# Value products of a half batch in two long runs instead of four, and one output projection for four batches, in a 16-head cross-attention on Trainium2

## The reference, cut to what matters

```
q = (x @ Wq.T).reshape(b, t, h, s)
k_ = (context @ Wk.T).reshape(b, tc, h, s)
v = (context @ Wv.T).reshape(b, tc, h, s)
dot = einsum('bthd,bchd->bhtc', q * e ** (-0.25), k_ * e ** (-0.25))
attn = softmax(dot, axis=-1)
out = einsum('bhtc,bchd->bthd', attn, v).reshape(b, t, e)
return out @ Wo.T + bo
```

## Time and profile before

| | us |
|---|---|
| median of 3 runs | 2212.78 |
| lowest and highest run | 2210.36 and 2214.60 |
| span of the profiled execution | 2210.2 |
| PE busy in it | 2062.2 (93%) |
| DVE busy in it | 1482.6 (67%) |
| ACT busy in it | 1200.2 (54%) |

### The profile page before, as it was taken

The page is one execution under the profiler, slowest core; times in us unless marked ns, Lnnn a source line. Parts: engine busy times, 40 slices in busy tenths (PEclk is TensorE's granted clock), DMA queues, the critical chain, the costliest instruction groups (busy, mean ns, idle before and its releaser), DMA issues. The chain is left out here.

```text
span 2210.2 us, 47308 instructions
## 1 busy us (share of the span) xinstructions
PE 2062.2 (93%) x18797; PEld 1505.9 (68%) x18797; DVE 1482.6 (67%) x3068; ACT 1200.2 (54%) x2313; POOL 752.7 (34%) x337
## 2 busy tenths in 40 slices
PE   5999999866999899999999999999997799999996
PEld 3677777655887455677777777777764457777774
DVE  5677777688986554566666666666626577777774
ACT  5877887634766222344444444444421467777763
POOL 6565566016875470112111211112000254433410
PEclk8999999967999898999999999999997889999997
DMA  6554544233540311231112211131000354544420
GB/s 161 148 148 132 159 134 132 63 85 97 143 136 20 79 38 39 70 104 66 60 60 82 97 60 60 60 100 62 1 1 25 87 159 126 149 126 139 122 79 9
DMA packets 94541, 199.78 MB, mean 90 GB/s; under 512 B 42113, under 2 KB 50353, under 8 KB 94066
## 3 DMA queue, kind: packets, MB, share of 16 engines
q1 hardware_dynamic: 94322, 196.75, 30.3%
HBM read 116.22 MB, written 0.65 MB: 53 GB/s over the span
## 5 line engine op out<-in xcount | busy, mean ns | idle before, releaser
L1630 PEld LDWEIGHTS L2ps<-L2probsT,L2values 125*128 125x128 f32 (+1 forms) x2688 | 317.4, 192 | 51.3 <-issue 48.9
L1611 PE MATMUL L2ps<-L2keys,L2qz 128*128 128x501 f32 x672 | 340.2, 590 | 0.9 <-DVE L2out_bias L1847 0.9
L1630 PE MATMUL L2ps<-L2probsT,L2values 125*128 125x128 f32 (+1 forms) x2688 | 318.5, 275 | 0.5 <-ACT L2probsT L1740 0.5
L1725 POOL TENSOR_TENSOR L2keys<-L2keys,L2mean_spread 127x1500 f32<-127x1500 f32 x15 | 50.9, 3395 | 583.0 <-DMA L2wqk<-L_moments 583.0
L1823 DVE CUSTOM_DVE_ANT_0 L2work<-L2ps,L2maskadd,L2big 128x1503 f32<-128x1503 f32 x112 | 199.5, 1781 | 72.9 <-PE L2ps L1611 72.7
L1625 PEld LDWEIGHTS L2ps<-const,L2work 128*126 128x126 f32 x1344 | 164.3, 140 | 118.7 <-issue 116.5
L654 ACT ACTIVATE L3probsT<-L3ps 128x448 f32<-128x448 f32 x384 | 196.0, 547 | 71.1 <-PE L3ps L511 66.5
L654 ACT ACTIVATE L0probsT<-L0ps 128x448 f32<-128x448 f32 x384 | 198.1, 551 | 47.7 <-PE L0ps L511 46.6
L1625 PE MATMUL L2ps<-const,L2work 128*126 128x128 f32 x1344 | 202.8, 273 | 3.5 <-DVE L2work L1832 3.1
L1742 ACT COPY L2qz<-L2ps 128x128 f32<-128x128 f32 x112 | 29.7, 265 | 304.7 <-PE L2ps L1630 304.7
L798 DVE TENSOR_REDUCE L0partmax<-L0ps 112x1 f32<-112x1000 f32 x128 | 153.4, 1199 | 58.1 <-PE L0ps L484 56.0
(11 more groups left out here) (479 smaller groups left out, 4164.7 us busy)
## 6 DMA issues: line engine op xcount, KB each, us to landing
L0key_stack<-L0key_parts SPq DMA_DIRECT2D x192, 187.5 KB
L3key_stack<-L3key_parts SPq DMA_DIRECT2D x192, 187.5 KB
L0ctxT<-in_ctxT SPq DMA_DIRECT2D x16, 750.0 KB, 4.4
L1rawT<-in_ctxT SPq DMA_DIRECT2D x16, 750.0 KB, 6.5
L2raw<-in_ctx SPq DMA_DIRECT2D x16, 750.0 KB
L3ctxT<-in_ctxT SPq DMA_DIRECT2D x16, 750.0 KB, 4.4
L2mean_spread<-L_moments SPq DMA_DIRECT2D x15, 750.0 KB, 6.7
L2wqk<-L_moments SPq DMA_DIRECT2D x15, 750.0 KB, 8.4
```

The source lines that it names most:

```text
L1611: last = nc.tensor.matmul(PS[:, 3 * (m % 2) + c, 0:NPR], tile_rows(m), KT[:, m // RT % 2, 500 * c:500 * c + NPR], start=True, stop=True)
L1630: last = nc.tensor.matmul(PS[:, bank, 0:P], V[0:keys_in(c), i // RT % 2, c, :], PT[0:keys_in(c), i % 2, c, :], start=c == 0, stop=c == NCH ...
```

## The change

`values` now does six chunks instead of three, and only in odd steps: half a batch's twelve chunks come in two runs of 24 matmuls each instead of four runs of 12. `pv_done` counts finished half batches instead of quarters. Y takes four batches at once, 224 columns instead of 56, in one step of every fourth batch (t = 0, b = 5, 9, 13 and 17); `Am` has room for four batches and lies in the space of the loaded weights `W`, which aren't needed any more by then. `copy_sums` now stands behind all the exponentials of its step instead of behind the first.

```diff
@@ of_step
-        if t == 0 and 0 <= b - 2 < B:
-            own.append(("Y", b - 2, 0, "D"))
+        if t == 0 and b % 4 == 1 and 0 <= b - 5 < B:
+            own.append(("Y", (b - 5) // 4, 0, "D"))
@@ tiles
-        Am = sb("heads_out", [P, 2, TT])
-        W = sb("w", [P, 6, P])
+        W = sb("w", [P, 7, P])
+        Am = W[:].rearrange("p a n -> p (a n)").rearrange("p (h x b q) -> p h x b q", h=2, x=2, b=4)
@@ values
-                wait_emptied(pe, plan.emptied("S", 4 * h + 3, (3 * part + 2) // 4))
+                wait_emptied(pe, plan.emptied("S", 4 * h + 3, part + 1))
-                for c in range(3 * part, 3 * part + 3):
+                for c in range(6 * part, 6 * part + 6):
-                last.then_inc(s.pv_done, 1)
+                if part == 1:
+                    last.then_inc(s.pv_done, 1)
@@ unit, Y on PE
-                    wait_emptied(pe, plan.emptied("R", 2 * i + 1, 0))
+                    wait_emptied(pe, plan.emptied("R", 8 * i + 7, 0))
-                            last = nc.tensor.matmul(PS[:, bank, 0:Q], WO[:, h, x, :], Am[:, h, x * Q:(x + 1) * Q],
+                            last = nc.tensor.matmul(PS[:, bank, 0:4 * Q], WO[:, h, x, :], Am[:, h, x].rearrange("p b q -> p (b q)"),
@@ PE's steps
-                h, part = n // 4 - 1, n % 4
-                if 0 <= h < HB:
-                    values(h, part)
+                if n % 2 == 1 and 0 <= n // 4 - 1 < HB:
+                    values(n // 4 - 1, n % 4 // 2)
@@ ACT's steps
                 for u in own[:1]:
                     empty(*u)
+                for u in own[1:]:
+                    empty(*u)
                 if n % 4 == 3 and 0 <= n // 4 - 1 < HB:
                     copy_sums(n // 4 - 1)
-                for u in own[1:]:
-                    empty(*u)
@@ Y on DVE
-                    x = k.xT[:, i * Q:(i + 1) * Q]
-                    nc.vector.scalar_tensor_tensor(x, PS[:, bank, 0:Q], bout[:], x, ALU.add, ALU.add
+                    x = k.xT[:, 4 * i * Q:4 * (i + 1) * Q]
+                    nc.vector.scalar_tensor_tensor(x, PS[:, bank, 0:4 * Q], bout[:], x, ALU.add, ALU.add
```

More of the change, by code:

```diff
@@ L435, in stack @@
                                  ).then_inc(stacked[slot], 16)
-            sp.dma_start(W[:], src[name + "_attn_w"]).then_inc(s.w_loaded, 16)
+            sp.dma_start(W[:, 0:6, :], src[name + "_attn_w"]).then_inc(s.w_loaded, 16)
             load_context(0)
@@ L652, in empty @@
                     if h >= 2 and tau == 0 and j == 0:
-                        act.wait_ge(s.pv_done, 4 * h - 4)
+                        act.wait_ge(s.pv_done, h - 1)
                     ins = nc.scalar.activation(PT[:, h % 2, 4 * j:4 * j + 4, tau, :],
@@ L666, in empty @@
                     if i >= 2:
-                        act.wait_ge(s.pv_done, 8 * i - 8)
+                        act.wait_ge(s.pv_done, 2 * i - 2)
                     act.wait_ge(s.ones_ready, 4)
@@ L703, in copy_sums @@
             def copy_sums(h):
-                act.wait_ge(s.pv_done, 4 * h + 4)
+                act.wait_ge(s.pv_done, h + 1)
                 if h >= 2:
@@ L782, in empty @@
                     link(nc.vector.reciprocal(PS[:, bank, 0:TT], PS[:, bank, 0:TT]))
-                    nc.vector.tensor_tensor(Am[:, i % 2, :], OS[:, i % 2, :], PS[:, bank, 0:TT], ALU.mult
-                                            ).then_inc(s.emptied_d, 1)
+                    b = i // 2
+                    nc.vector.tensor_tensor(Am[:, i % 2, :, b % 4, :], OS[:, i % 2, :].rearrange("p (x q) -> p x q", x=2),
+                                            PS[:, bank, 0:TT].rearrange("p (x q) -> p x q", x=2), ALU.mult).then_inc(s.emptied_d, 1)
                 elif what == "Y":
-                    x = k.xT[:, i * Q:(i + 1) * Q]
-                    nc.vector.scalar_tensor_tensor(x, PS[:, bank, 0:Q], bout[:], x, ALU.add, ALU.add
+                    x = k.xT[:, 4 * i * Q:4 * (i + 1) * Q]
+                    nc.vector.scalar_tensor_tensor(x, PS[:, bank, 0:4 * Q], bout[:], x, ALU.add, ALU.add
                                                    ).then_inc(s.emptied_d, 1)
```

## The result

The changed kernel takes 2222.34 us (median of 6 runs, 2212.21 to 2224.00); the kernel before takes 2213.69 us (median of 6, 2209.05 to 2216.34) beside it. The ratio is 1.0037, with a 95% interval of 1.0019 to 1.0055: slower by about 8.7 us. The forecast was 2224.

What follows compares the result with a forecast made beforehand. PE, busy 349.3 of 350 us at full clock, was taken to set the time. Terms per layer -15.1 + 20.4 + 2.1 + 3.6 - 7.2 + 1.9 = +5.7, two layers +11.4 us, gave 2224 us; range 2209 to 2234.

Steps and rivals of the forecast that it cites:

- The wait that this uncovers: Before `scores12` in even steps, PE waits for DVE's 1.92 us loop: 30 times 0.68, +20.4 us per layer.
- the end of the layer: From n = 120 on, where ACT's exponentials set the pace from n = 122: +1.9 us per layer.
- Half as many runs: Value runs merged in 58 pairs per layer, 0.26 us saved per pair: -15.1 us per layer.
- M: M at t = 2 waits for the row maxima, 0.15 us more in 14 batches: +2.1 us per layer.
- Sums later: R at t = 4 waits 0.3 us for the later sums copy in 12 batches: +3.6 us per layer.
- Y for four: At t = 0, 14 Ys of 0.90 us leave and three of 1.52 come, plus the last: -7.2 us per layer.
- The last batches and the end: +0.4 us at n = 120, then +1.5, an estimate between 0 and 3, from n = 122: +1.9 per layer.
- PE's sum decides everywhere: Faster rival: the 1.92 us loop before `scores12` does not bind, so less PE work saves time; 2165 us, chance 0.08.
- No change: Rival: the `scores12` wait exists, but M, R and the end of the layer cost nothing; 2209 us, chance 0.17.
- t = 4 and t = 6 wait too: Slower rival: those even steps also wait, 28 more waits per layer of 0.3 us; 2241 us, chance 0.09.

Runs made afterwards that it cites:

- e3_short_max: Changed kernel with `max12` reading 500 of its 1000 columns; 2195.26 us, ratio to the kernel before 0.9926.
- e5_runs_only: Kernel before with only the two long value runs; sums copied early and Y per batch as before; 2227.72 us, ratio 1.0062.
- e2_sums_early: Changed kernel with the copy of the sums back behind the first exponentials; 2209.55 us, ratio to the kernel before 0.9987.
- e1_y4_only: Kernel before with only Y done for four batches at once; short runs and early sums kept; 2204.79 us, ratio 0.9974.
- e9_spread4: Changed kernel with sums copied early, K at t = 1, 3, 4, V at t = 5, 6, 7 and a fourth context buffer; 2180.32 us.
- e10_before_spread4: Kernel before with K at t = 1, 3, 4, V at t = 5, 6, 7 and a fourth context buffer; 2207.23 us, ratio 0.9972.

## Why the prediction was right

**The wait that this uncovers** was the term that decided, and it came as worked out: C to C 1.92 us, 0.48 us idle (forecast about 0.5), at t = 0 and t = 2 in batches 1 to 14 and at t = 4 in batches 13 and 14, 31 times a layer: the 30 counted and the one at n = 120, which the prediction has under the end of the layer. That is 30.0 us in both layers where 30 were forecast. `e3_short_max` shows that it is the cause: with the loop short, the loss becomes a gain, while the same edit in the kernel before gives 3 us.

**Half as many runs and M**: the two and the wait together +0.47 worked, +0.44 measured (`e5_runs_only`). M starts at 205.57, which is 2.93 after C; 2.94 was worked out.

**Sums later**: 0.3 a batch forecast, 0.37 in L0 and 0.28 in L3 measured. R waits 12 times for the copy in L0, though the view shows 0.2 us each and not 0.3; in L3 it puts the 0.2 on the weight load and on ACT's exponentials instead. At t = 0 it is hidden, as said: batches 13 and 14 are the same with the sums early.

**Y for four**: `e2_sums_early` has (3 x 24.04 + 25.55) / 4 = 24.42 against 24.93 with a Y per batch, -0.51; worked -0.52. One Y adds 1.52 to its batch, and its eight passes take (176.03 - 174.45) / 8 = 0.20 us each:

```profile
174.45 1.74 PE L534 MATMUL L0ps<-L0w,L0w_out 128*128 128x224 f32 x8
176.03 0.37 PE L529 MATMUL L0ps<-L0osum,L0select_sums 128*128 128x112 f32 x2
```

By the formula of the Trainium skill ("TensorE: Matmul & The Clock Gate", Back-to-back issue gap), an estimate, 224 columns take 96 ns. The trace differs, and it decides. But Y's term holds only where it was put in the sum, behind the long runs: in the kernel before (`e1_y4_only`) Y's removal gives 0.48 and not 0.90, because the reciprocal's chain on DVE ends last at t = 0. In the kernel after, PE stands still at t = 0 for `max12` anyway, and DVE has caught up by then.

**The last batches and the end**: batch 13 went from 21.84 to 23.60, batch 14 from 21.85 to 22.08. Worked: 3 x 0.68 + 0.15 - 4 x 0.26 + (1.52 - 0.90) = 1.77 and 3 x 0.68 + 0.15 - 1.04 - 0.90 = 0.25; measured 1.76 and 0.23. From the `scores0` of n = 120 to the first matmul of the last Y a layer takes 22.59 where it took 21.55, +1.04. With the Y of that step gone (0.90 by the earlier trace rows), the end cost 1.94 where 1.9 was put; but 1.5 of it was a guess between 0 and 3, so that it came so close is luck.

In all, +5.7 us a layer was forecast, and 5.8 and 4.4 came. L3 lacks 0.09 a batch of the late sums, 1 us; of the rest of its difference about half lies ahead of batch 1 and half behind n = 120. That L0 came out to 0.1 us is in part luck too, since misses of up to 0.6 us partly cancel: it is 0.58 longer ahead of n = 0, batch 0 is shorter by 1.07 and not 0.52, batch 1 longer by 0.41 and not 0.77 (before the change its 24.01, without Y, already held the wait behind the reciprocal that `e1_y4_only` shows), and batches 2 to 12 longer by 2.23 and not 1.61. PE's busy time was forecast as 333 of 350 us and is 330.5 and 331.5.

**The rivals.** For "PE's sum decides everywhere" the sign would have turned at a loop of 1.73 us; it was 1.92. Given other work in the short steps, it came true in the body of L3 (`e9_spread4`), to 0.03 us a batch. Its 2165 us was not reached: L0 still waits for ACT, and in batches 13 and 14, without K, the waits are back (22.96 in batch 13 against 21.85 before). "No change" would have needed M, R and the end of the layer at nothing; R alone costs 3.4 to 4.4 us a layer. Its sum has a slip: with half of the three it comes to 2217 and not 2213, and with Y at 0.90 the 2209 falls to 2204, outside the range and not at its edge. "t = 4 and t = 6 wait too" did not happen: no `scores12` of batches 1 to 12 waits there. At t = 4 it follows without a gap, 210.97 - 208.80 = 2.17 after the C before:

```profile
208.80 0.63 PE L484 MATMUL L0ps<-L0key_stack,L0query_stack 97*112 97x500 bf16 x2
...
210.97 0.59 PE L484 MATMUL L0ps<-L0key_stack,L0query_stack 97*112 97x500 bf16 x2
```

## What to carry to other kernels

A term of "work saved on the busiest engine" is worth its time only as long as each step stays longer than the loop through another engine that its single buffer makes; so write down that loop (here bank, maximum, bank: 1.92 us) beside the shortest step (2.08) before bundling work into fewer steps, and expect the bundled kernel to need its other work spread over the steps that became short. When work is moved between steps, follow the buffers that it frees: a unit one step later here held back a load, and one more buffer turned a loss of 1.3% into a gain of 1.4%.

## What the runs showed of the hardware

The same instructions at L2's start ran at a granted clock of 0.60 over 20 us in one execution and 1.00 in another, both behind 20 us of unbroken PE work at 1.00 and a gap on PE of 2.95 us; this moved L2's first score matmuls by 6.4 us, over half of what the change costs. The 53.6 us of the kernel before stand in ten of the twelve profiles, the 47.2 in those of the kernel after and of `e5_runs_only`. It doesn't look like a property of a kernel: the other five runs of the kernel after have a lower mean clock than its profile, and the ten runs of `e2_sums_early` and of `e10_before_spread4` spread over 0.952 to 0.959. Nor does the mean clock tell it: the profile of `e5_runs_only` has 0.953, as that of before, because it is at the lower level longer elsewhere (around L3's start, for one). What decides between the two was not found. So profiles are compared by their stages, and times by several runs.
